# One pool of five PSUM banks placed by an estimate of when each is free, convolution pieces weighed by a step's other work, and copies of P and V moved to ScalarE

## What is computed

```python
y = einsum('bthk,btkhd->bthd', softmax(x @ Wl.T + bl), x_windows) + bias
z = selu(conv1d(y, Wc, 31 taps, VALID) + bc);  h = z @ W2.T + b2      # 375 -> 345 tokens
h = h + attention0(layernorm(h))     # softmax((q+u)k + (q+v)pos) @ v, 8 heads of 64
h = h + experts0(layernorm(h))       # top 2 of 8, 256 hidden, plus a shared expert
h = h + linear_attention(layernorm(h))
h = h + experts1(layernorm(h))       # groups, top 8 of 64, capacity 256
```

## Time and profile before

| | us |
|---|---|
| median of 3 runs | 2902.91 (2899.16 to 2906.61) |
| the profiled execution, its own time | 2928.45 |
| its span | 2926.8 |
| PE / DVE / ACT / POOL busy | 2099.7 / 1572.0 / 786.9 / 752.2 |
| granted TensorE clock, mean | 0.906 |

### The profile page before, as it was taken

One profiled execution on the slowest core, in us unless ns is written; L12 is line 12 of the kernel. 1 busy time (PEld: TensorE's weight loads), 2 busy tenths in 40 slices (PEclk: granted clock), 3 DMA queues, 4 the chain that ended last, 5 costly groups with the idle time before them and its releaser, 6 DMA issues. The chain is left out here.

```text
span 2926.8 us, 48566 instructions
## 1 busy us (share of the span) xinstructions
PE 2099.7 (72%) x16960; PEld 1636.7 (56%) x16960; DVE 1572.0 (54%) x4618; ACT 786.9 (27%) x1921; POOL 752.2 (26%) x624
## 2 busy tenths in 40 slices
PE   1357958888888787887888878878888777516671
PEld 1246746766666666666666666766666545413340
DVE  2347435665655565565556565656556665523441
ACT  0133314233323232233232323332322332102120
POOL 1000000004040403040213121304040440466885
PEclk9878979999999999999999999999999999757775
DMA  3344743224132323232223222312130000005774
GB/s 105 131 169 178 252 160 99 90 76 122 60 104 75 111 60 92 70 109 62 77 72 99 72 71 68 102 59 78 58 92 1 8 7 1 9 6 121 116 114 64
DMA packets 171218, 250.28 MB, mean 86 GB/s; under 512 B 71401, under 2 KB 126639, under 8 KB 169852
## 3 DMA queue, kind: packets, MB, share of 16 engines
q10 hardware_dynamic: 43672, 153.59, 16.7%
q0 software_dynamic: 61584, 49.12, 8.1%
q1 hardware_dynamic: 65732, 44.55, 5.6%
HBM read 202.50 MB, written 86.53 MB: 99 GB/s over the span
## 5 line engine op out<-in xcount | busy, mean ns | idle before, releaser
L923 PE MATMUL Cb<-seq_hi,ring 128*128 128x174 f16 x4544 | 635.7, 246 | 55.6 <-DVE conv_s L1581 19.2
L923 PE MATMUL Cb<-seq_lo,ring 128*128 128x174 f16 x2272 | 543.9, 246 | 0.0
L836 POOL TENSOR_TENSOR rstd<-ve,minus_half 115x3 f32<-115x3 f32 x64 | 70.1, 1095 | 1695.3 <-DVE ve L1624 990.2
L848 POOL DMA_INDIRECT slots_dram<-rows,slot_i x384 | 456.2, 1188 | 133.8 <-issue 133.8
L1873 DVE TENSOR_REDUCE nmax<-W 115x1 f32<-115x345 f32 x384 | 197.7, 515 | 529.9 <-PE W L923 396.3
L923 PEld LDWEIGHTS Cb<-seq_hi,ring 128*128 128x128 f16 x4544 | 421.2, 101 | 87.9 <-DVE seq_lo L1560 21.1
L1400 ACT ACTIVATE area_h<-W,nmax 115x345 f32<-115x345 f32 x384 | 210.5, 548 | 854.8 <-DVE nmax L1873 770.8
L923 PE MATMUL W<-area_k,qv 128*115 128x345 f32 x768 | 307.3, 483 | 60.0 <-ACT area_h L1400 45.9
L923 PE MATMUL W<-mx_hl,w_hl 128*128 128x345 f16 x960 | 202.3, 328 | 121.3 <-DVE area_h L1794 116.9
L1096 PEld LDWEIGHTS W<-ident,area_h 115*115 115x115 f32 x1152 | 166.5, 184 | 154.2 <-ACT area_h L1400 38.9
L923 PEld LDWEIGHTS Cb<-seq_lo,ring 128*128 128x128 f16 x2272 | 228.7, 101 | 23.7 <-issue 3.5
(11 more groups left out here) (227 smaller groups left out, 3201.0 us busy)
## 6 DMA issues: line engine op xcount, KB each, us to landing
ring<-filters_dram ACTq DMA_DIRECT2D x252, 512.0 KB
filters_dram<-ring ACTq DMA_DIRECT2D x36, 512.0 KB, 5.7
slots_dram<-in_empty_slots POOLq DMA_DIRECT2D x8, 1544.0 KB, 14.2
area_k<-slots_dram SPq DMA_DIRECT2D x64, 193.0 KB
band<-band_dram SPq DMA_DIRECT2D x64, 182.1 KB
slots_dram<-rows,slot_i POOLq DMA_INDIRECT x384
qv<-in_wc POOLq DMA_DIRECT2D x2, 1984.0 KB, 9.8
area_h<-in_wc POOLq DMA_DIRECT2D x2, 1984.0 KB, 14.4
```

The source lines that it names most:

```text
L836: pool.tensor_tensor(rstd[g][:, :], ve[g][:, :], minus_half[:, :], ALU.pow)\
L848: pool.indirect_dma_start(out=slots_d, out_offset=bass.IndirectOffsetOnAxis(ap=slot_i[:, m:m + 1], axis=0), in_=rows[:, m // 8, :], in_off ...
L923: return pe.matmul(o, l, r, start=start, stop=stop)
```

## The change

1. `W` has five banks and there is no `Ob`. `place` walks through all uses of a full iteration with an estimated time each, and gives each to the bank that an estimate (`KEEPS`, us that a use keeps a bank) has free first. `FREED` names the reader as before.
2. `plan` weighs a point by what else TensorE has there: `step_load` estimates it, and a step's weight is (3.3 - load) / 0.077, at least 2. The front has 24, 4, 4. Inside a group pieces follow the weights; before they were even. `TAIL_STEP` is 17 instead of 18.
3. ScalarE copies all units of P and the three blocks of V; VectorE none. `kv_ready` is split into `k_ready` and `v_ready`; TensorE waits for V at the first pair of heads, no longer ahead of step 0.
4. VectorE does `hidden` at the end of the same step, ahead of the next `nmax`; `gate_weights` moves from step 0 to projection point 13, and the exponential of the gate on ScalarE to point 12.
5. Layer 1's parts (`LATE_PART`) skip steps 3 and 14, so the last ones stand one or two steps later.
6. In setup the convolution goes by whole filter chunks, and the mixing of sequences 2 and 3 starts ahead of chunks 5 and 18, one part for each chunk.

```diff
-weight_of = [12, 12, 20] + [7] * len(PROJ) + [11.5] * UNITS + [8] * 4
-PAIR_WEIGHTS = [8] * HEAD + weight_of + weight_of[:FRONT + len(PROJ) + TAIL_STEP]
+def step_load(s):
+    t = 0.63 * (s < UNITS) + 0.32 * (1 <= s <= UNITS) + 2.5 * (pair_at(s, 2) is not None) + 1.36 * (s in DOWN_AT)
+    return t + (0.45 if HID_AT.get(s, NHID) < 2 * E0 else 0.9 if s in HID_AT else 0)
+STEP_US, CONV_US = 3.3, 0.077
+weight_of = [24, 4, 4] + [7] * len(PROJ) + [max(2, (STEP_US - step_load(s)) / CONV_US) for s in range(STEPS)]
+PAIR_WEIGHTS = weight_of[POINTS - HEAD:] + weight_of + weight_of[:FRONT + len(PROJ) + TAIL_STEP]
...
-MIX_FROM = {2: 16, 3: 44}
+MIX_FROM = {2: 5, 3: 18}
+SOFTMAX_AT = {2: 4} | {tb + 1: first + 2 * TILES + LAG + 1 for tb, first in MIX_FROM.items()}
+BANDS_AT = {first + n + LAG: (tb, n) for tb, first in MIX_FROM.items() for n in range(2 * TILES)}
...
+LATE_PART = {s: n for n, s in enumerate(s for s in range(26) if s not in (3, 14))}
...
+PROJ_US, KEEP_STEP = 1.7, 4.0
+KEEPS = {"ln": 3, "out0": 2, "q": 1.5, "k": 2.5, "v": 2, "gate0": 2, "S": 2.5, "T": 3, "hid": 4, "sg": 5, "su": 5,
+         "N": 4.5, "O": 9, "Y": 5}
...
 def place(uses, banks):
-    for n, u in enumerate(uses):
-        b = n % banks
+    free, where = [0.0] * banks, {}
+    for use, t in uses:
+        b = min(range(banks), key=lambda n: free[n])
+        free[b] = max(free[b], t) + KEEPS[use[0]]
+        where[use] = b
...
-        W = [ctx.enter_context(nc.psum_tensor(f"W{i}", [128, 512], F32)) for i in range(3)]
+        W = [ctx.enter_context(nc.psum_tensor(f"W{i}", [128, 512], F32)) for i in range(BANKS)]
-        Ob = [ctx.enter_context(nc.psum_tensor(f"Ob{i}", [128, 512], F32)) for i in range(2)]
...
@@ ScalarE
+                    if ro.a is not None and name == "v":
+                        bank = wait_full(act, ro, ("v", h))
+                        act.activation(V[:, h, :], bank[0:A, :], ACT.Copy).then_inc(v_ready.h, 1)
-                    if ro.a is not None and 1 <= s <= UNITS and (s - 1) % 2 == 0:
+                    if ro.a is not None and 1 <= s <= UNITS:
@@ VectorE, in a step
-                    if ro.f is not None and s - 1 in HID_AT:
-                        hidden(ro, HID_AT[s - 1])
-                    if ro.a is not None and 1 <= s <= UNITS and (s - 1) % 2 == 1:
-                        dve.tensor_copy(pt_of(u), bank[0:A, 0:TOK].rearrange("p (i a) -> p i a", i=J))\
-                    if ro.f is not None and s == 0:
-                        gate_weights(ro)
                     conv_at(ro, STEP0 + s)
+                    if ro.f is not None and s in HID_AT:
+                        hidden(ro, HID_AT[s])
```

More of the change, by code:

```diff
@@ L186, in w_uses @@
         if attends and s < UNITS:
-            out.append(("S", s))
+            out.append((("S", s), t))
         if attends and 1 <= s <= UNITS:
-            out.append(("T", s - 1))
+            out.append((("T", s - 1), t + 0.7))
         if mixes and s in HID_AT:
-            out += hid_uses(HID_AT[s])
+            out += [(u, t + 1.2) for u in hid_uses(HID_AT[s])]
         if attends and pair_at(s, 2) is not None:
[L193 to L202, removed]
+            out += [((name, pair_at(s, 2)), t + 2.5) for name in "ON"]
@@ L220, with count @@
+    return where
+def count(uses, where):
+    seen, out = [0] * BANKS, {}
+    for use, _ in uses:
+        seen[where[use]] += 1
+        out[use] = (where[use], seen[where[use]])
+    return out, seen
+BANKS = 5
 KINDS = {"first": (1, 0), "full": (1, 1), "last": (0, 1)}
-W_AT = {kind: place(w_uses(*k), 3) for kind, k in KINDS.items()}
-O_AT = {kind: place(o_uses(*k), 2) for kind, k in KINDS.items()}
-W_PER, O_PER = W_AT["full"][1], O_AT["full"][1]
+W_BANK = place(w_uses(1, 1), BANKS)
+W_AT = {kind: count(w_uses(*k), W_BANK) for kind, k in KINDS.items()}
@@ L224 @@
+W_PER = W_AT["full"][1]
 C_USES = [("group", o, n) for o in range(OC) for n in range(len(GROUPS))] + [("w2", r) for r in range(2)]
-C_AT = place(C_USES, 2)[0]
+C_AT = {use: (n % 2, n // 2 + 1) for n, use in enumerate(C_USES)}
 assert len(C_USES) % 2 == 0
@@ L551, in bank_of @@
         def bank_of(ro, use):
-            at, banks, full = (W_AT, W, w_full) if use in W_AT["full"][0] else (O_AT, Ob, o_full)
-            i, nth = at[ro.kind][0][use]
-            return banks[i], full[i], full[i].at(ro.b, nth)
+            i, nth = W_AT[ro.kind][0][use]
+            return W[i], w_full[i], w_full[i].at(ro.b, nth)
         def wait_full(eng, ro, use):
@@ L562, in wait_freed @@
         def wait_freed(eng, ro, use):
-            ats, order = (W_AT, w_uses) if use in W_AT["full"][0] else (O_AT, o_uses)
-            at = ats[ro.kind][0]
-            uses = order(*KINDS[ro.kind])
+            at = W_AT[ro.kind][0]
+            uses = [u for u, _ in w_uses(*KINDS[ro.kind])]
             prev = next((v for v in reversed(uses[:uses.index(use)]) if at[v][0] == at[use][0]), None)
@@ L571, in wait_freed @@
                     return
-                older = ats[ro.before][0]
-                prev = next(v for v in reversed(order(*KINDS[ro.before])) if older[v][0] == at[use][0])
+                older = W_AT[ro.before][0]
+                prev = next(v for v, _ in reversed(w_uses(*KINDS[ro.before])) if older[v][0] == at[use][0])
                 ago = 1
@@ L1152, in conv_at @@
                 for ahead, p in conv_points(ro.parity, at):
-                    conv(ro.pair if ahead == 0 else ro.next_pair, p)
+                    k = ro.pair if ahead == 0 else ro.next_pair
+                    if k is not None and p < len(PLAN):
+                        conv(k, BEGIN[p], BEGIN[p + 1])
             def iteration(ro):
@@ L1468, in _ @@
                     load_filters(1, i + RING)
+                for name, o in events_at(p, ACT_EVENTS):
+                    conv_event(1, name, o)
             every_batch(act, iteration)
-            for s in range(UNITS):
+            for s in range(STEPS):
                 late(B - 1, s)
@@ L1865, in iteration @@
                         gate_logits(ro)
+                    if ro.f is not None and r == GATE_AT + 4:
+                        gate_weights(ro)
                     conv_at(ro, FRONT + r)
@@ L1995, in _ @@
             phases_split(1)
+            for p in range(HEAD):
+                for name, o in events_at(p, DVE_EVENTS):
+                    conv_event(1, name, o)
             for part in range(2):
```

142 lines of the change are left out of this document (62 added, 80 removed).

## The result

The changed kernel takes 2653.0 us (median of 4, 2644.6 to 2653.7) against 2904.8 for the one before in the same comparison: ratio 0.9127, 95% interval 0.9102 to 0.9153. The profiled execution is 2653.7 us with a span of 2652.0, so 275 us of span are to be explained (before: 2926.8).

The account below looks back on a forecast made before the run. The loop was taken as bound by TensorE's order: its work plus waits, mostly for `hidden`. Terms -128 - 6 - 6 - 15 - 9 - 12 + 15 + 10 + 12 = -139 us, from 2902.9 to 2764 us; range 2690 to 2885.

Parts of the forecast that it names:

- Bank depth grows only a little. The larger part is the moved `hidden`: Iterations 2 to 13: of the 170.4 us of PE waits for `hidden`, the earlier product removes more than the five banks.
- I keep a quarter of the waits: Iterations 2 to 13: busy DVE in about a quarter of the steps keeps that share of 170.4 us; gain -128 us.
- So nothing is charged: Loop steps: `hidden` ahead of `nmax` costs nothing; ring about 2.5 us, step about 3.6, 1 us to spare.
- The price of a wait: PE's wait for `hidden` in the loop: 0.82 us for one, 170.4 us as the sum in iterations 2 to 13.
- the clock's: Iterations 2 to 13: fewer idle stretches return a fifth of up to 57 us lost at the lower clock, -12 us.
- +15: Front of iterations with bands: fewer convolution pieces there uncover waits for bands, 1.5 us in each of ten iterations.
- +10: Later iterations' steps with few pieces, and four S uses at short bank distances: +10 us over twelve iterations, bounds 0 and 30.
- `seq_lo`'s 9 us: Iterations 2 to 13: the split of the next pair's sequence is done with a step to spare, -9 us.
- Copies: P and V copies moved from DVE to ScalarE, with `gate_weights` leaving step 0, take 40% of exponential waits: -15 us.
- C, the slower rival: Loop banks: wrong time estimates make PE wait at 25 uses at distance four or less; about 3025 us, chance 0.12.
- Elsewhere: Outside iterations 2 to 13: iteration 1 -6 us, last iterations -6, setup with iteration 0 +12.
- B: Rival: all 170.4 us of `hidden` waits, the 36.5 for the exponential and most clock loss go; about 2680 us, chance 0.08.

Follow-up runs that it names:

- flat keeps: Changed kernel with every use estimated to keep its bank 3 us, only O 9, instead of an estimate for each kind of use: 2648.5 us, ratio 0.9116.

## Why the prediction was wrong

**Where it looked was right.** The kernel was bound by PE's order, and the waits for `hidden` were the thing to remove: iterations 2 to 13 carry 240 of the 275 us. For them -139 was forecast. Of the 101 us that are missing, PE's idle time makes 61 (-188 against -127) and its busy time 40 (-52 against -12).

**"Bank depth grows only a little. The larger part is the moved `hidden`"** is the step that failed on the cause. I compared averages, three or four against five. What mattered is that a plain step has just three `W` uses, S, T and hid. So with three banks in turn the bank of each of the 16 hidden blocks was taken again three uses later, in the next step or the one after: nine times by the next hidden block, three times by S, three by T, once by sg. DVE's product stood behind `nmax` of the step after. At a distance of four or five the late product holds few: 59 us of waits are left of 170. Alone the pool gave 5.7%, the move 4.1%, and onto the pool the move adds 0.4%. No run tells the match of three banks with three uses from the short distance as such.

**"I keep a quarter of the waits"**: 43 us were kept, 14 stayed. That is 28 of the 101.

**"So nothing is charged" for the moved `hidden`** holds for `nmax`, and left out O's division behind the product: 19.1 us of PE's waits in iterations 2 to 13, of which 3.6 are left with the late product.

**The price of a wait** was taken as its row. In the earlier trace rows the row says 0.82, but turn to hidden block is 1.28 us (1194.35 to 1195.63), and 0.30 without a wait in the changed kernel (1195.82 to 1196.12): the wait cost 0.98. The turn of before:

```profile
1194.35 0.47 PE L1096 MATMUL W<-ident,area_h 115*115 115x115 f32 x3
```

It is shown with 0.47 us in both kernels. Without a wait the last 0.17 of that overlap the next block; ahead of a wait they stand alone and count as busy. Over 17 profiles (all but those three from the faster chip, below) a fit gives PE's busy time in these iterations as 1301 us + 0.23 for each wait + 0.38 for each us at the lower of the two clock levels, and misses none by more than 5.4. With 164 waits and 34 us at the lower clock fewer (126 to 92) it gives -37 and -13; measured -52. The fit is no experiment, but its 0.23 is near the 0.17 of the one wait read above. The term was absent from the forecast, and the clock's was about right (-12).

**"+15" and "+10" for the plan** were too dear, and the whole has the wrong sign. I priced what pieces uncover in the front and in thin steps, and took only `seq_lo`'s 9 us as gain. Undone it costs 1.6%, some 48 us; alone it gives 2.3%. The waits for bands grew from 7.9 to 12.4 us, all waits at tile L from 33.5 to 39.2. What I left out is that pieces in light steps are cover: with the plan undone the waits for the exponential are 45 us instead of 18. A wait of 16.5 us for SELU's read of the bank, which I did not count at all, is gone too, but not by the plan alone: undone, 3.7 us come back, and in the kernel with only the copies it is already 7.9.

**Copies**: -15 forecast, 0.8% or 23 us measured both ways; the size is about right. The way is not shown: the forecast took them from the waits for the exponential, and these carry 6 of the 23. A V copy on ScalarE is 595 ns, of which I had taken 650. The advice of the Trainium skill for VectorE ("ScalarE: Activation LUTs", Rules for kernel authors), given for bf16 and weighed in the prediction, would have lost here; fp32 copies from PSUM are shorter on ScalarE in both sizes, 451 to 513 and 595 to 689 ns.

**C, the slower rival**, was not the outcome, but its mechanism is real: one use ahead of a bank still held stops all of PE. It does not go by the 25 near uses. Of these one waits in each iteration, Y4, three behind a score (12 waits, 3.9 us); the large wait is the one for O's bank, ten uses back. With flat keeps it is Y's reader, with four banks the exponential.

**Elsewhere**: iteration 1 -12 (-6 forecast), the last iterations -21 (-6), setup and iteration 0 -2 (+12). Setup's band wait grew as said, from 9.80 us to 16.49, yet setup got shorter by 5 us; among kernels that share the changed setup it is 281 to 292 us, against 294.8 before.

**The result has about B's size by another road.** B had 2680 with the clock coming back; the clock hardly moved (0.96 to 0.97).

What stays open: parts of the overlap beyond pool and early product (plan and copies add 2.1% onto those two, and 3.1% as the sum of each alone) were not separated. A placement that keeps sg off O's bank was not run.

## What to carry to other kernels

Compare the rotation of banks with the period of the work: here, with as many banks in turn as a plain step has uses, the bank of every hidden block came round again within two steps, mostly before its late reader was done (163 waits in twelve iterations). Write down for each pair of uses of a bank how far apart they are and what the first one's reader waits for, and what stands ahead of that reader on its engine: a slow reader behind a far use can cost more than a near one (17.8 us at ten uses, 3.9 at three). The mean distance tells little. When several edits aim at one wait, forecast them as substitutes, give filler work a value wherever a step is light, and expect a wait of TensorE to cost more than its row.

## What the hardware showed that I had not expected

PE's busy time, as the profile shows it, is no constant of the work: nearly the same matmuls took 1350 to 1420 us in iterations 2 to 13. By the fit, waits (117 to 281) and the time at the lower clock (58 to 160 us) explain up to some 38 us each.

Chips differ. On one the kernel before takes 2845.6 us, on others 2898 to 2931; part of the spread among the others is not the chip's, as one of them gave 2922.7 at one time and 2898.3 at another. One kernel, the one with more pieces in the front, ran on two of them: spans 2617.0 and 2663.2 us, with the same duration of each VectorE and ScalarE group. The slower shows idle time on DVE ahead of the maximum put down to "remote", a release that the profile can't name. On the faster chip no wait of DVE or ACT is put down to it, in three profiles; on the others it is 64 to 148 us for each of the two engines. Faster chip:

```profile
L1891 DVE TENSOR_REDUCE nmax<-W 115x1 f32<-115x345 f32 x384 | 196.8, 512 | 261.6 <-PE W L935 227.5 <-issue 26.2 <-DVE h L1829 4.9
```

Slower chip:

```profile
L1891 DVE TENSOR_REDUCE nmax<-W 115x1 f32<-115x345 f32 x384 | 196.9, 513 | 266.9 <-PE W L935 212.6 <-issue 31.0 <-remote 17.5
```

What it is wasn't found. Ratios are alike on both (0.9186 and 0.9182), so parts are compared here by ratios. Waits in us are not comparable with the faster chip: the same kernel has 98.7 us of them there and 130.1 on the slower.
